# One batch of sixteen gets its moments on ScalarE, and GpSimd sums six batches of sixteen instead of five

## What is computed

```python
def reference(x, adj, bias, gumbel):
    h = relu(layernorm(x))                   # over the last axis, biased variance, eps 1e-5
    x_avg = h.transpose(2, 0, 1).mean(1)     # (N, T): the mean over the 64 batches
    x_norm = x_avg / max(norm(x_avg), 1e-12)
    sim = (x_norm @ x_norm.T + 1) / 2
    a = sim + gumbel0 > 1 - sim + gumbel1    # (N, N)
    a_sym = clip(a + a.T, 0, 1);  nmask = clip(a_sym + eye, 0, 1)
    common = nmask @ nmask.T
    struct = where(a_sym * (common > 1) > 0, common / common.max() * common, 0)
    W = a * struct;  deg = W.sum(0)
    Wn = deg**-.5 [:, None] * W * deg**-.5 [None, :]
    xw = einsum('nbt,to->nbo', h, adj)
    return x + (einsum('sd,sbt->dbt', Wn, xw) + bias)   # back in (B, T, N)
```

## Time and profile before

| | us |
|---|---|
| median of three executions (lowest, highest) | 853.83 (852.73, 854.52) |
| the profiled execution | 853.35 |
| its span in the trace | 851.6 |
| busy in the span: TensorE, VectorE, ScalarE, GpSimd | 821.1, 583.3, 508.4, 309.3 |
| pass 1, to the start of S | 107.45 |
| from the start of S to the end of the span | 744.2 |

### The profile page before, as it was taken

The page is one execution under the profiler, slowest core; times in us unless marked ns, Lnnn a source line. Parts: engine busy times, 40 slices in busy tenths (PEclk is TensorE's granted clock), DMA queues, the critical chain, the costliest instruction groups (busy, mean ns, idle before and its releaser), DMA issues.

```text
span 851.6 us, 13546 instructions
## 1 busy us (share of the span) xinstructions
PE 821.1 (96%) x4739; PEld 429.6 (50%) x4746; DVE 583.3 (68%) x679; ACT 508.4 (60%) x530; POOL 309.3 (36%) x255
## 2 busy tenths in 40 slices
PE   4999999969999999999999999999999999999997
PEld 3545455554454555555455555554555455545553
DVE  7999986789986665666566666656665666566652
ACT  3888714879645665665566566656664555565531
POOL 4888710030433333333333333334333433333320
PEclk9999999989999999999999999999999999999999
DMA  8999913100553333333322223222222222233111
GB/s 346 408 409 345 421 46 124 50 1 1 214 183 126 106 109 107 124 106 108 103 99 99 99 99 99 99 99 99 99 99 99 99 99 99 99 101 111 60 50 74
DMA packets 30121, 113.14 MB, mean 133 GB/s; under 512 B 3472, under 2 KB 3600, under 8 KB 29072
## 3 DMA queue, kind: packets, MB, share of 16 engines
q1 hardware_dynamic: 30096, 112.80, 36.6%
HBM read 79.23 MB, written 33.55 MB: 132 GB/s over the span
## 4 chain that ended last, share of the span: by engine, by line
PE 80%; DVE 13%; issue 3%; ACT 2%; DMA 1%; DVEq 0%; SPq 0%; ACTq 0%
PE ps L852 65%; PE ps L795 8%; DVE stats L944 8%; PE ps L867 2%; PE ps L813 1%; PE ps L667 1%; DVE moments L950 1%; PE ps L724 1%; DMA out_dram<-obuf 1%; DVE ybuf L965 1%; DVE xring L1007 1%; DVE obuf L1198 1%; DVE ybuf L1042 0%; PE ps L738 0%; PE ps L731 0%
## 5 line engine op out<-in xcount | busy, mean ns | idle before, releaser
L852 PE MATMUL ps<-a,ybuf 128*128 128x512 f16 x2604 | 570.9, 379 | 0.5 <-ACT obuf L522 0.5
L852 PEld LDWEIGHTS ps<-a,ybuf 128*128 128x128 f16 x2604 | 252.6, 98 | 295.6 <-ACT obuf L522 1.0
L1042 DVE TENSOR_TENSOR ybuf<-zbuf,ybuf 128x1024 f16<-128x1024 f32 x124 | 164.5, 1327 | 157.4 <-ACT ybuf L508 157.4
L380 POOL TENSOR_TENSOR zbuf<-zbuf 128x512 f32<-128x512 f32 x31 | 40.9, 1318 | 444.1 <-ACT zbuf L489 444.1
L508 ACT ACTIVATE ybuf<-zbuf 128x1024 f16<-128x1024 f32 x124 | 117.8, 950 | 115.4 <-POOL zbuf L385 99.9
L522 ACT ACTIVATE obuf<-ps,bias_sb,w_out 128x512 f32<-128x512 f32 x62 | 47.9, 772 | 116.9 <-PE ps L852 111.7
L1031 DVE TENSOR_TENSOR hring<-hring 128x1024 f16<-128x1024 f32 x56 | 68.5, 1224 | 55.8 <-ACT hring L469 55.8
L795 PEld LDWEIGHTS ps<-w,hring 128*128 128x128 f16 x1344 | 79.5, 98 | 14.9 <-issue 2.4
L795 PE MATMUL ps<-w,hring 128*128 128x128 f16 x1344 | 84.2, 219 | 1.9 <-ACT zbuf L489 1.5
L1198 DVE TENSOR_TENSOR obuf<-obuf,xring 128x1024 f32<-128x1024 f32 x64 | 80.4, 1258 | 2.7
L383 POOL TENSOR_TENSOR zbuf<-zbuf 128x512 f32<-128x512 f32 x31 | 68.8, 2220 | 0.0
(11 more groups left out here) (133 smaller groups left out, 673.1 us busy)
## 6 DMA issues: line engine op xcount, KB each, us to landing
xring<-in_x_dram SPq DMA_DIRECT2D x96, 512.0 KB, 4.6
out_dram<-obuf SPq DMA_DIRECT2D x64, 512.0 KB, 2.9
ybuf<-in_x_dram SPq DMA_DIRECT2D x28, 512.0 KB, 8.3
a<-in_L_gnn_gumbel_dram SPq DMA_DIRECT2D x7, 1024.0 KB, 15.9
obuf<-in_x_dram SPq DMA_DIRECT2D x11, 512.0 KB, 5.7
obuf<-in_L_gnn_gumbel_dram SPq DMA_DIRECT2D x1, 1024.0 KB, 23.9
w<-in_adj_dram SPq DMA_DIRECT2D x1, 64.0 KB, 1.9
bias_sb<-in_L_gnn_bias_dram SPq DMA_DIRECT2D x1, 0.5 KB, 2.1
```

What stands on the lines that cost most here:

```text
L852: mm = nc.tensor.matmul(bank[q % 2], y16[:, q % 2, yk, u, c * P:(c + 1) * P], a16[:, ak, mat, c, :], start=(start and c == yk == ak == 0), ...
L1042: nc.vector.tensor_tensor(y16[:, q % 2, 1, a:a + n, :], z[:, a + 1:a + 1 + n, :], y16[:, q % 2, 0, a:a + n, :], ALU.subtract).then_inc(s_y, 1)
```

## The change

Three things change, all in pass 1. `POOL_SUMS` gains j = 10, so GpSimd adds six batches in trips 0 to 2 and TensorE ten instead of eleven; the last trip is written out by hand and keeps its adds. VectorE leaves out the moments of j = 11. ScalarE makes these in `moments_of`, between relu 2 and relu 3 of the same trip: a copy with scale 1/N whose accumulated output is the mean, a step on one column that gives minus the mean times N^-1/2, and a square of (x - mean) / N^1/2 whose accumulated output is the variance. The full outputs go to PSUM banks 4 and 5, which nobody reads. Each of the three waits for the one before. Before norm 3, GpSimd waits for VectorE's moments of the group and for these.

```diff
-POOL_SUMS = (0, 3, 6, 8, 12)
+POOL_SUMS = (0, 3, 6, 8, 10, 12)
+SCALAR_STATS = 11
+STATS_AFTER = 3
...
+        minus_mean = sb("minus_mean", [P, 1])
...
+        ps_dump = pair[2]
...
-                pool.wait_ge(s_mom, BODY1 * i + a + n)
+                pool.wait_ge(s_mom, (BODY1 - 1) * i + a + n - (SCALAR_STATS < a + n))
+                if a <= SCALAR_STATS < a + n:
+                    pool.wait_ge(s_amom, 3 * i + 3)
...
+            def moments_of(i, j):
+
+                act.wait_ge(s_x1[j], 16 * (i + 1))
+                act.wait_ge(s_norm, NG * i + norm_group(j) + 1)
+                nc.scalar.activation(ps_dump, x1[j], ACT.Copy, scale=1.0 / N,
+                                     accum_out=moments[:, j, 0:1]).then_inc(s_amom, 1)
+                act.wait_ge(s_amom, 3 * i + 1)
+                act.sem_inc(s_bnseen, 1)
+                nc.scalar.activation(minus_mean[:], moments[:, j, 0:1], ACT.Copy, scale=-N ** -0.5).then_inc(s_amom, 1)
+                act.wait_ge(s_amom, 3 * i + 2)
+                act.sem_inc(s_bnseen, 1)
+                nc.scalar.activation(ps_dump, x1[j], ACT.Square, bias=minus_mean[:, 0:1], scale=N ** -0.5,
+                                     accum_out=moments[:, j, 1:2]).then_inc(s_amom, 1)
+
             def relus(i, except_for=()):
                 for j in range(BODY1):
+                    if j == STATS_AFTER:
+                        moments_of(i, SCALAR_STATS)
                     if j not in except_for:
                         relu1(i, j)
...
                 for q in range(BODY1 // 2):
-                    for j in (2 * q, 2 * q + 1):
+                    mine = [j for j in (2 * q, 2 * q + 1) if j != SCALAR_STATS]
+                    for j in mine:
...
-                    dve.wait_ge(s_bn, 2 * (BODY1 * i + 2 * q) + 4)
+                    dve.wait_ge(s_bn, 2 * ((BODY1 - 1) * i + 2 * q + len(mine) - (SCALAR_STATS < 2 * q)))
                     dve.sem_inc(s_bnseen, 1)
-                    for j in (2 * q, 2 * q + 1):
+                    for j in mine:
                         nc.vector.bn_aggr(moments[:, j, :], stats[:, j % 4, :]).then_inc(s_mom, 1)
```

More of the change, by code:

```diff
@@ L187, in gnn_kernel @@
         s_mom = sem("moments_ready")
+        s_amom = sem("moments_of_scalar_engine")
         s_pchain = sem("pool_chain")
```

## The result

| | before | after |
|---|---|---|
| median (lowest, highest), us | 854.05 (852.73, 854.52) | 866.62 (866.23, 868.77) |
| profiled execution, its span | 853.35, 851.6 | 866.96, 865.2 |
| start of S | 107.45 | 120.36 |
| from there to the end of the span | 744.2 | 744.8 |
| busy: TensorE, VectorE, ScalarE, GpSimd | 821.1, 583.3, 508.4, 309.3 | 822.0, 577.6, 517.9, 317.6 |

After over before is 1.0153, with a 95% interval of 1.0133 to 1.0174; the median before is now of four executions. Of the 13.6 us between the two spans 12.9 stand ahead of S. VectorE has 5.7 us less to do, ScalarE 9.5 and GpSimd 8.3 more; the sums of busy time tell the reader nothing of which of these shows.

The account below looks back on a forecast made before the run. The prediction took GpSimd to bound pass 1 (23.5 us a trip; VectorE and TensorE 22.5). Delays summed to +11.3 us at S, on the profiled 853.35 giving 864.65; it said 864.9 us, range 859 to 870.

Parts of the forecast that it names:

- GpSimd sets the pace, the chain view is a trap: Pass 1: GpSimd paces at 23.5 us a trip, though the profile's chain of waits names VectorE, at 22.5.
- VectorE as the bound: Rival, pass 1: VectorE is the bound after all, so 5.6 us of moments go, 847.8 us; chance 0.05.
- The sixth add: GpSimd's queue, trips 0 to 2, behind add(8): 2.53 us each, three times 7.6 us, with no cover.
- The block: ScalarE's moments between relu 2 and relu 3, four times: 2.6 us each, bounds 2.2 and 3.5.
- the 1.5 us that I had named for it: ScalarE's passes writing PSUM: if its lower latency helped, the sum would be some 1.5 us lower.
- Trip 0: First trip: ScalarE's moments wait for x[11], landing at 19.7, so norm 3 starts at 26.0 instead of 24.00: 2.0 us.
- Trips 1 to 3: add(3) waits for relu 3: 0.9 us late in trips 1 and 2 (0.7 net each), 1.6 in trip 3.
- Norm 3 of the last trip: GpSimd, last trip: late by 7.6 + 1.4 + 1.6 + 2.0 = 12.6 us.
- The end: End of pass 1: GpSimd's last norm 0.3 to 1.5 us quicker, L965 slowed beside add(6), S later by 11.3 us.
- the alternative that I had priced as *cheaper: End of pass 1: if L965 escapes running beside GpSimd's add(6), the delay is +9.6 us instead of +11.3.
- After S the same length: Behind S: from there to the end the same length as before, as pass 2 is the same code.
- The rival that TensorE slows: Rival: gaps let TensorE restart at 1.2 GHz, two batches behind relu 15 end 3 us late, 868 us; chance 0.12.

Follow-up runs that it names:

- block_after_relu3: Changed kernel with ScalarE's moments of j = 11 moved from ahead of relu 3 to behind it; ratio 1.0105 to the kernel before.
- sixth_add_alone: Kernel before with only j = 10 moved from TensorE's sums to GpSimd's; ratio 1.0079 to the kernel before.
- short_add: Kernel before with GpSimd's add of j = 8 cut to 16 columns of 1024; ratio 1.0015 to the kernel before.
- merged_norm: Kernel before with the last two norm groups of a trip joined into one; ratio 1.0004 to the kernel before.
- block_of_15: Changed kernel with ScalarE making the moments of j = 15, ahead of relu 12, instead of j = 11; ratio 1.0130 to the kernel before.
- no_block_at_end: Kernel before with last two norm groups joined, x[11] loaded early, ScalarE's j = 11 moments behind relu 3 in trips 0 to 2 only; ratio 0.9957.

## Why the prediction was right, point by point

- *GpSimd sets the pace, the chain view is a trap.* Right for work that is added: the add alone cost 7.07 us. VectorE's relief alone gained 1.20 (the 1.09 of trip 0's wait and 0.26 at the end, summed to 1.35 by the rows), where VectorE as the bound would have given over 4. But GpSimd's relief alone gained 0.05, so for work that is taken away the chain view, which ended on VectorE, named the engine with the little that there was to gain.
- *The sixth add*, 2.53 us each: 2.49 to 2.50 by the trace.
- *The block*, 2.6 us: 2.73. Short by the term of ScalarE's own waits, taken as 0.03 from VectorE; they are 0.12 and 0.13 (74.86 to 74.98, 75.18 to 75.31). The Square at 1.12 and the column step at 0.20 were sized right. The first pass writes PSUM in 1.00 to 1.03 us, against 1.06 for the pass of the earlier trace rows into SBUF. That is the direction of the Trainium skill's rule (ScalarE: Activation LUTs, Step-by-step: what each stage is for) that PSUM is the quicker destination. But the two differ in function and input type as well (a Copy of f32 here, a Square of f16 there), and no run changes the destination alone, so the rule is not shown, and the 1.5 us that I had named for it did not come.
- *Trip 0*: the load landed as dated (19.7; the block started at 19.84), norm 3 at 26.35 instead of 26.0, with load and block each 0.1 us longer than forecast.
- *Trips 1 to 3*: 0.9, 0.9 and 1.6 late, forecast; by the steps from add(0) to add(3) it is 1.1, 1.1 (4.41 before, 5.53 after in trip 2) and 1.7.
- *Norm 3 of the last trip*: +12.6 forecast, +13.24 measured (93.59 to 106.83), which is these small terms added up.
- *The end* was the step that failed. I had GpSimd's last norm quicker by 0.3 to 1.5 us, add(6) at 111.2, and L965 caught beside it. In fact the steps of both last norms ran beside VectorE's closing operations: from the start of norm 4 to add(6) it is 5.90 us (108.63 to 114.53), where it was 4.48 (95.39 to 99.87). The last norm's first step took 1.23 us instead of 0.2, just as long as VectorE's add that began 0.05 us before it. The control is in block_after_relu3: there norm 4, beside VectorE, took 2.48 us as here, and norm 5, with VectorE idle, 1.47 where it is 3.42 here. Add(6) came at 114.53, L965 (now L989) escaped it (0.81), and L1007 waited 2.59 for the sum. The price is +12.9 instead of +11.3: the alternative that I had priced as *cheaper* (+9.6) happened, but with its other half, the late add, unpriced. So it is not quite true that, as the opening has it, the engines wait for each other only at semaphores. The trace agrees here with the Trainium skill (GPSIMD Engine Reference, Key points), which has GpSimd and VectorE contend for the SBUF interfaces that they share when VectorE's instruction has two SBUF inputs or runs in a 2-port performance mode; which mode VectorE's one-input steps ran in, no trace here shows. In block_after_relu3 it was the other way about: VectorE's L1002 took 3.25 us beside the add, against 1.23.
- *After S the same length*: 744.8 against 744.2, nearly.
- *The rival that TensorE slows* came true in part, at no cost ahead of S and a small one behind it. Behind a wait of 2.23 us four pieces took 3.68 us, not 1.88:

```profile
94.31 3.68 PE L719 MATMUL ps<-zbuf,ident 128*128 128x512 f32 x4 [2.23 <-ACT zbuf L419]
97.83 1.88 PE L719 MATMUL ps<-obuf,ident 128*128 128x512 f32 x4
```

The granted clock of 85 to 105 us was 0.91, a mix of the 1.2 and 2.4 GHz levels. But TensorE has 5 us of room a trip now, and its last sum was done at 119.3, ahead of S. Behind S the matmuls that broadcast the norms took 3.62 us, where they took 2.96 before, and the first comparison of the graph started 10.4 us behind S instead of 9.7. The sum of the prediction, 864.65, missed the profiled 866.96 by 2.3 us: 1.6 up to S, and the 0.7 of these matmuls. The forecast owes its fit to the terms up to norm 3 of the last trip, and these are not luck. In the end of the pass two misses partly cancel: a collision that was forecast (L965 beside the add, some 2.2 us) stayed away, and one that was not (the slow norms) came.

## What to carry to other kernels

Where several engines need nearly the same time a round, find the one that waits for nobody in the middle of the loop. Relief given to another is worth at most the waits for it; load laid on the pacing one, even through an operation of a third engine that its next step needs, shows in full beyond the slack ahead of that step. Read the loop's first and last rounds by themselves: here a load not yet landed and a hand-written last trip decided 2.5 and 5.3 us. Where a delay shifts two engines against each other, look at which of their instructions now run side by side: that was the term that the forecast lacked. And test relief in pairs, since two engines that hide each other show nothing one at a time.

## What the runs showed of the hardware that I had not expected

The code behind S is the same in all these kernels, yet its length in the profiled executions varied from 742.0 to 748.1 us (the table), more than some effects under test. A part of it lies in the first microseconds. TensorE's timeline just behind S, first in sixth_add_alone, then in short_add, last in the changed kernel (the column sums of S squared, then the matmuls that broadcast the norms):

```profile
115.92 1.95 PE L710 MATMUL ps<-ones,hring 128*128 128x1 f32 x16 [0.72 <-ACT hring L437]
...
119.32 2.27 PE L672 MATMUL ps<-ident,rnorm 128*128 128x128 f32 x16 [0.68 <-POOL rnorm L375]
```
```profile
108.80 2.85 PE L711 MATMUL ps<-ones,hring 128*128 128x1 f32 x16 [3.96 <-ACT hring L438]
...
112.93 3.62 PE L673 MATMUL ps<-ident,rnorm 128*128 128x128 f32 x16
```
```profile
121.77 1.95 PE L733 MATMUL ps<-ones,hring 128*128 128x1 f32 x16 [0.70 <-ACT hring L460]
...
125.17 3.62 PE L695 MATMUL ps<-ident,rnorm 128*128 128x128 f32 x16 [0.68 <-POOL rnorm L382]
```

In the first, the granted clock of 115 to 125 us was 1.00, the 2.4 GHz level, and the first comparison of the graph started 9.0 us behind S. In the second, that of 110 to 115 us was 0.50, the 1.2 GHz level, and the comparison started 11.1 us behind S. TensorE had idled 3.96 us there before the column sums, as it had ended its own sums early; the two other kernels with slow column sums (merged_norm, 2.92 us, and block_of_15, 3.57) had idled 2.24 and 2.20 us, and the eleven others, with 0.84 us or less, have 1.95 or less. So a kernel that lets TensorE finish early can lose behind S, as short_add does: its S is where it was, its comparison 1.4 us later, its median 1.6.

The idle time just before is not the whole cause. The changed kernel has the same short waits as sixth_add_alone, yet its broadcast ran at 3.62 us, with a granted clock of 0.66 in 125 to 130 us. And in its trips, a wait of 2.24 us before 67.39 was followed by four pieces in 1.98 us, one of 2.23 before 94.31 by the 3.68 above. Nor do the first microseconds explain all of the length: no_block_at_end also started its comparison 9.0 us behind S, and has 744.4 us to the end. What decides the clock there stays open; no experiment here changed the idle time alone.
